# A fused attention and feed-forward layer: the five engines' instruction lists in a new order

## The reference

```python
x = x + xcond(layernorm(x), ctx, ctx, k_length)     # 8 heads, softmax over the 256 columns
x = x + ffn(layernorm(x), w_router, w_fc, w_proj)   # two experts, top one by a router

def xcond(q, k, v, k_length):
    s = SCALE * log(k_length)[:, None, None, None]
    attn = softmax(s * einsum('bhdq,bhdk->bhqk', qh, kh))
    return einsum('bhqk,bhdk->bhdq', attn, vh)

def ffn(x, w_router, w_fc, w_proj):
    logits = x @ w_router.T                           # 2 experts
    a = square(where(h >= 0, h, 0.5 * h))             # h = x @ w_fc[e].T, 1024 wide
    return a @ w_proj[e].T                            # of the chosen expert, times its probability
```

## Time and profile before

| | |
|---|---|
| median of 3 runs | 172.38 us (172.37 to 172.74) |
| profiled execution, span of its instructions | 170.4 us (its own time is not given apart from the three runs) |
| TensorE, busy | 161.4 us (95%) |
| VectorE, busy | 129.2 us (76%) |
| ScalarE, busy | 97.0 us (57%) |
| GpSimd, busy | 58.6 us (34%) |
| ACT_TABLE_LOAD | 1 of 1.28 us |

### The profile page before, as it was taken

How to read it: one execution, slowest core, us unless ns; L and a number is a source line. 1 busy time by engine, 2 the same in 40 slices (tenths; PEclk the granted TensorE clock), 3 DMA queues, 4 the chain that set the end, 5 groups by cost and what they waited for, 6 DMA issues and landing times.

```text
span 170.4 us, 4075 instructions
## 1 busy us (share of the span) xinstructions
PE 161.4 (95%) x1494; PEld 139.9 (82%) x1494; DVE 129.2 (76%) x301; ACT 97.0 (57%) x181; POOL 58.6 (34%) x68
## 2 busy tenths in 40 slices
PE   7998887899999989999989999999999999999992
PEld 7986745487698869896978798969879999999991
DVE  7799987999898999995999867953179875056442
ACT  4444979558659956957346526943794065335220
POOL 7331544630322420372521260405023253136330
PEclk9999999999999999999999999999999999999999
DMA  4577857794468054004501460002010000010001
GB/s 120 167 241 246 259 190 233 217 292 126 143 229 251 3 161 120 14 19 139 174 0 62 125 189 4 0 0 67 0 62 0 4 0 0 4 61 0 0 4 62
DMA packets 18883, 16.98 MB, mean 100 GB/s; under 512 B 1776, under 2 KB 18672, under 8 KB 18864
## 3 DMA queue, kind: packets, MB, share of 16 engines
q1 hardware_dynamic: 18144, 16.00, 30.3%
q10 hardware_dynamic: 720, 0.73, 1.5%
HBM read 8.72 MB, written 1.05 MB: 57 GB/s over the span
## 4 chain that ended last, share of the span: by engine, by line
PE 75%; DVE 11%; issue 4%; SPq 3%; ACT 3%; DMA 2%; DVEq 0%; ACTq 0%
PE hp L1358 25%; PE ops L1388 22%; PE pv L1342 6%; PE stp L1318 6%; PE ops L1273 5%; DVE negm L813 5%; PE snp L1265 3%; DMA x_raw<-x 2%; ACT probs L514 2%; DVE a_lo L921 2%; PE ops L1376 2%; PE pv L1376 1%; PE stp L1324 1%; PE pv L1398 1%; PE snp L1301 1%
## 5 line engine op out<-in xcount | busy, mean ns | idle before, releaser
L378 POOL TENSOR_TENSOR a_buf<-l_buf 128x512 f32<-128x512 f32 x32 | 35.7, 1119 | 77.8 <-DVE a_lo L921 44.6
L514 ACT ACTIVATE probs<-stp,scale_b 128x1024 f32<-128x1024 f32 x30 | 33.4, 1114 | 14.8 <-PE stp L1318 11.3
L1358 PE MATMUL hp<-xt_hi,wfc_hi 128*128 128x256 f32 x128 | 37.2, 291 | 0.0
L813 DVE TENSOR_REDUCE negm<-snp 128x4 f32<-128x1024 f32 x28 | 34.1, 1218 | 3.6 <-PE snp L1265 3.4
L1358 PE MATMUL hp<-xt_hi,wfc_lo 128*128 128x256 f32 x128 | 35.8, 279 | 0.0
L1358 PE MATMUL hp<-xt_lo,wfc_hi 128*128 128x256 f32 x128 | 35.7, 279 | 0.0
L522 ACT ACTIVATE l_buf<-hp 128x512 f32<-128x512 f32 x32 | 18.8, 594 | 23.7 <-PE hp L1358 17.0
L921 DVE TENSOR_TENSOR a_lo<-a_buf,a_hi 128x512 fp32r<-128x512 f32 x32 | 26.2, 831 | 7.6 <-ACT a_hi L529 6.2
L1358 PEld LDWEIGHTS hp<-xt_hi,wfc_hi 128*128 128x128 f32 x128 | 24.0, 188 | 2.1 <-issue 1.0
L1388 PE MATMUL ops<-wproj_hi,a_hi 128*128 128x256 f32 x112 | 23.6, 292 | 0.5 <-DVE wproj_lo L953 0.5
L1358 PEld LDWEIGHTS hp<-xt_hi,wfc_lo 128*128 128x128 f32 x128 | 24.1, 188 | 0.0
(11 more groups left out here) (112 smaller groups left out, 237.2 us busy)
## 6 DMA issues: line engine op xcount, KB each, us to landing
k_st<-k_hi SPq DMA_DIRECT2D x16, 128.0 KB, 2.1
wfc_raw<-w_fc_t SPq DMA_DIRECT2D x8, 256.0 KB, 4.4
wproj_raw<-w_proj_t SPq DMA_DIRECT2D x8, 256.0 KB, 3.5
q_st<-q_hi SPq DMA_DIRECT2D x14, 128.0 KB, 2.1
x_raw<-x SPq DMA_DIRECT2D x8, 128.0 KB, 3.0
k_st<-k_lo SPq DMA_DIRECT2D x8, 128.0 KB, 2.4
v_raw<-ctx_t SPq DMA_DIRECT2D x8, 128.0 KB, 2.6
x_keep<-x SPq DMA_DIRECT2D x8, 128.0 KB, 2.7
```

The lines of the kernel that those rows point to most:

```text
L378: pool.tensor_tensor(a_buf[d % 2][:, :, :], l_buf[d % 2][:, :, :], l_buf[d % 2][:, :, :], ALU.mult).then_inc(s_a, 1)
L514: act.activation(probs[g][:, :, :, :], pair[:, :, :].rearrange("p e (c n) -> p e c n", c=KC), ACT.Exp, scale=scale_b[:, b:b + 1]).then_inc ...
L813: dve.tensor_reduce(negm[b % 2][:, :, :, g].rearrange("p c e -> p e c"), pair[:, :, :].rearrange("p e (c n) -> p e c n", c=KC), AX.X, ALU. ...
L1358: last = pe.matmul(hp[:, d % 2, half], wfc[w][:, kc, c * P:(c + 1) * P], xt[:, kc, :], start=(c % 2 == 0 and kc == 0 and w == 0 and xt is ...
```

## The change

The entries of all five lists stand in another order; each entry stands in it once, as before. The core of the difference, by engine:

```diff
 # ACT
-            act.preload_act_table_set("natural_log_exp_and_others")
+            load_consts()
             load_kv(act, 0)
-            load_consts()
             load_kv(act, 1)
+            load_router()
             k_part_hi(0)
             x_ln(0)
             x_rstd(0)
             q_part_hi(0)
             x_ln(1)
+            len_log()
             x_rstd(1)
+            q_put()
             k_part_hi(1)
-            q_put()
+            k_part_hi(2)
             q_part_hi(1)
...
             max_rows(0)
             x_ln(2)
             x_rstd(2)
+            x_ln(3)
+            x_rstd(3)
             exp(0, 0)
-            x_ln(3)
-            split_w(0, 1)
-            x_rstd(3)
+            split_w(0, 2)
             exp(0, 1)
...
+            max_rows(1)
+            pick_keys()
+            k_part_hi(3)
             split_w(0, 3)
-            exp(0, 3)
+            x_ln(4)
+            x_rstd(4)
+            x_ln(5)
+            x_rstd(5)
+            exp(1, 0)
+            exp(1, 1)
+            exp(1, 2)
+            exp(1, 3)
+            y_ln(0)
+            y_rstd(0)
...
+            act.preload_act_table_set('natural_log_exp_and_others')
             leaky(3, 6)
+            square_hi(3, 6)
             leaky(3, 7)
-            square_hi(3, 6)
             square_hi(3, 7)
 # DVE
+            q_normalise(1)
             q_put()
-            q_normalise(1)
             row_max(0, 0)
 # PE
+            values(2, 0)
+            values(2, 1)
+            scores_qk(3, 3)
             ffn1(0, 0)
             ffn1(0, 1)
-            scores_kq(2, 3)
-            scores_qk(3, 3)
-            values(2, 0)
-            values(2, 1)
 # SP
             load_x(sp, 0)
             load_x(sp, 1)
+            load_weights(sp, 0, 0)
+            keep(0)
             stack_k(sp, 0, 0)
```

More of the change, by code:

```diff
@@ L572, in _ @@
             x_rstd(2)
+            x_ln(3)
+            x_rstd(3)
             exp(0, 0)
-            x_ln(3)
-            split_w(0, 1)
-            x_rstd(3)
+            split_w(0, 2)
             exp(0, 1)
+            exp(0, 2)
             q_part_hi(2)
-            split_w(0, 2)
-            exp(0, 2)
-            split_w(0, 3)
-            exp(0, 3)
+            q_part_hi(3)
+            exp(0, 3)
+            max_rows(1)
+            pick_keys()
+            k_part_hi(3)
+            split_w(0, 3)
+            x_ln(4)
[8 more added lines that the diff above has]
+            y_rstd(0)
             split_w(0, 4)
             split_w(0, 5)
[L585 to L591, removed]
             split_w(0, 6)
             q_part_hi(4)
[L594 to L600, removed]
             max_rows(2)
             split_w(0, 7)
-            x_rstd(5)
-            x_ln(6)
             exp(2, 0)
+            split_w(1, 0)
             y_ln(1)
@@ L608, in _ @@
             exp(2, 1)
+            k_part_hi(4)
+            k_part_hi(5)
+            exp(2, 2)
             xt_part_hi(0)
[L610 to L613, removed]
             exp(2, 3)
+            split_w(1, 1)
+            split_w(1, 2)
+            x_ln(6)
             leaky(0, 0)
             square_hi(0, 0)
-            q_part_hi(5)
[L618 to L622, removed]
+            max_rows(3)
+            leaky(0, 1)
+            square_hi(0, 1)
+            exp(3, 0)
+            split_w(1, 3)
+            q_part_hi(5)
             leaky(0, 2)
[L624 to L627, removed]
+            x_rstd(6)
             exp(3, 1)
             leaky(0, 3)
-            coef_exp(0)
-            split_w(1, 3)
-            square_hi(0, 3)
             exp(3, 2)
-            k_part_hi(5)
+            square_hi(0, 2)
             leaky(0, 4)
             exp(3, 3)
+            square_hi(0, 3)
+            y_ln(2)
+            y_rstd(2)
+            coef_exp(0)
+            k_part_hi(6)
             max_rows(4)
-            y_ln(2)
-            k_part_hi(6)
             split_w(1, 4)
+            split_w(1, 5)
             leaky(0, 5)
-            y_rstd(2)
             square_hi(0, 4)
-            split_w(1, 5)
+            exp(4, 0)
             y_ln(3)
-            square_hi(0, 5)
             y_rstd(3)
+            k_part_hi(7)
             leaky(0, 6)
-            exp(4, 0)
-            square_hi(0, 6)
             exp(4, 1)
@@ L653, in _ @@
             q_part_hi(6)
+            exp(4, 2)
+            square_hi(0, 5)
+            square_hi(0, 6)
+            leaky(0, 7)
             split_w(1, 6)
-            leaky(0, 7)
+            leaky(1, 0)
+            exp(4, 3)
+            max_rows(5)
+            split_w(1, 7)
+            x_ln(7)
+            x_rstd(7)
             square_hi(0, 7)
-            leaky(1, 0)
-            exp(4, 2)
+            square_hi(1, 0)
+            exp(5, 0)
             leaky(1, 1)
-            k_part_hi(7)
@@ L661, in _ @@
[L661 to L664, removed]
+            square_hi(1, 1)
             leaky(1, 2)
-            square_hi(1, 1)
-            q_part_hi(7)
-            exp(5, 0)
             square_hi(1, 2)
             exp(5, 1)
-            leaky(1, 3)
             exp(5, 2)
             exp(5, 3)
+            leaky(1, 3)
+            q_part_hi(7)
+            leaky(1, 4)
+            square_hi(1, 3)
+            y_ln(4)
+            y_rstd(4)
@@ L674, in _ @@
+            leaky(1, 5)
             coef_exp(1)
             max_rows(6)
[L676 to L681, removed]
+            y_ln(5)
             square_hi(1, 4)
-            y_ln(5)
-            y_rstd(5)
             square_hi(1, 5)
             leaky(1, 6)
+            y_rstd(5)
+            exp(6, 0)
+            xt_part_hi(2)
+            leaky(1, 7)
             exp(6, 1)
-            xt_part_hi(2)
@@ L689, in _ @@
             square_hi(1, 6)
-            leaky(1, 7)
+            square_hi(1, 7)
             exp(6, 2)
-            square_hi(1, 7)
             exp(6, 3)
-            coef_exp(2)
[L695 to L705, removed]
+            leaky(2, 0)
+            square_hi(2, 0)
@@ L706, in _ @@
+            max_rows(7)
+            exp(7, 0)
+            leaky(2, 1)
+            square_hi(2, 1)
+            leaky(2, 2)
+            exp(7, 1)
+            exp(7, 2)
+            exp(7, 3)
+            square_hi(2, 2)
+            y_ln(6)
+            coef_exp(2)
+            y_rstd(6)
             leaky(2, 3)
+            square_hi(2, 3)
             leaky(2, 4)
[L708 to L711, removed]
             square_hi(2, 4)
@@ L714, in _ @@
             y_rstd(7)
+            leaky(2, 5)
             xt_part_hi(3)
+            leaky(2, 6)
+            coef_exp(3)
             square_hi(2, 5)
-            leaky(2, 6)
+            square_hi(2, 6)
             leaky(2, 7)
-            square_hi(2, 6)
+            square_hi(2, 7)
             leaky(3, 0)
-            square_hi(2, 7)
-            coef_exp(3)
             square_hi(3, 0)
@@ L1576, in _ @@
             ffn2(1, 4)
-            ffn1(1, 11)
             ffn2(1, 5)
@@ L1626, in _ @@
             ffn2(2, 3)
+            ffn2(2, 4)
+            ffn1(2, 10)
+            ffn1(2, 11)
             ffn1(2, 12)
-            ffn2(2, 4)
             ffn1(2, 13)
+            x_transpose(3)
             ffn1(2, 14)
             ffn1(2, 15)
-            x_transpose(3)
             ffn2(2, 5)
@@ L1638, in _ @@
             ffn1(3, 2)
+            ffn1(3, 3)
             ffn2(2, 8)
```

574 lines of the change are left out of this document (285 added, 289 removed).

## The result

The changed kernel takes **207.32 us** (four runs, 206.40 to 208.09) against 172.52 us for the kernel before in the same comparison: **1.201 times** as long, interval 1.195 to 1.207, some 35 us. The forecast was 199 with a range of 187 to 231. The profiled execution of the changed kernel is the one of 208.09 us.

What follows compares the result with a forecast made beforehand. The prelude's chain through all engines, then PE's feed-forward matmuls, were taken to bound the kernel; 18.3 (prelude) + 5.2 (later waits) + 3 (PE's speed) = 26.5 on 172.4 gave 199 us, range 187 to 231, own bounds 192 to 207.

Steps and rivals of the forecast that it cites:

- The count and the price of the loads: On ACT: 34 table loads instead of one, 1.28 us each, 1.48 with its activation; busy time from 97.0 to about 139.
- The prelude, steps 1 to 5: Chain from layer norm to first `ffn1`, in five stretches: first `ffn1` at 63.2 against an equal point of 44.9, +18.3 us.
- some 15: Part of the prelude's 18.3 us put down to the table loads in it, in us.
- the rest: Part of the prelude's 18.3 us beyond the loads' share, put down to the new order itself.
- step 1: From the start to the first `row_max`: loads around the first `x_ln`, `x_rstd` pairs move it from 8.61 to 14.2, +5.6 us.
- PE's speed: PE's matmuls in the prelude may run slower after long waits: 3 us taken, at best 0, at most 6.8.
- I find two such places: Under feed-forward work, PE waits at `x_transpose(1)` (1.9 us) and `x_transpose(3)` (3.3): together +5.2, between 0 and 8.
- DVE may be the later one anyway: At the two late transposes, DVE rather than ACT might set the time, the reason for a lower bound of 0.
- Each load holds ACT longer: Rival: up to 1.52 us more behind each load on ACT, some 22 x 1.4 = 31 us more, 230 us; chance 0.18.
- Only the prelude pays: Rival: loads under feed-forward work hide, PE keeps its speed and regains 1.2 us of gaps, 189.5 us; chance 0.12.
- Not slower: Rival: every load runs in ACT's 73.4 us of idle time, or loads are not run, 172 us; chance 0.04.

Runs made afterwards that it cites:

- the late loads alone: New order with the right table preloaded at ACT's head and `exp_and_others` preloaded behind `exp(2,3)`, against the kernel before: 1.076 times, median 186.66 us.

## Why the prediction was right, and where it was off

Begin of the landmarks, us from the start of the span; the last line is the first `ffn1` or the equal point:

| | before | predicted | one load, new order | changed | changed, 53 more fillers |
|---|---|---|---|---|---|
| first `row_max` | 8.61 | 14.2 | 9.47 | 13.73 | 13.73 |
| `exp(0,0)` | 15.80 | 26.4 | 16.57 | 29.44 | 25.84 |
| `exp(1,0)` | 25.61 | 41.4 | 27.11 | 47.36 | 41.61 |
| `exp(2,0)` | 37.40 | 52.6 | 38.91 | 59.87 | 53.71 |
| first `ffn1` | 44.9 | 63.2 | 49.02 | 71.14 | 64.98 |

- **The count and the price of the loads** were right: 34 of 1.28 us, ACT busy 140.8 (forecast 139), and 1.51 us for a load with its activation (forecast 1.48).
- **The prelude, steps 1 to 5,** was right as a mechanism and, with the clock kept at 1.00, in size: the last column differs from the forecast by at most 1.8 us, 20.1 against 18.3 at the first `ffn1`. Of these, 18.0 are the loads ("some 15"), 2.1 the order ("the rest"). At the first pair (step 1) the order's share, by the kernel with one load, is 9.47 - 8.61 = 0.9 us, the loads' 13.73 - 9.47 = 4.3.
- **PE's speed** was the first term that was mis-sized: forecast 3, "at best 0", at most 6.8; 3.5 to 6.2 was measured. In the changed kernel PE waits 3.6 us for `q_hi`, then up to 5.0 us for `probs`, its granted clock goes to 0.50, and ten fillers take 4.22 us instead of 2.50. The first fillers of the earlier trace rows, from which the forecast had its ratio of 224 to 128, were slow at a clock that reads 1.00; why, no run shows. The choice of 3 rested on half of the pieces being slow; all of them from 10 to 20 us are, in the profiled execution.
- **"I find two such places"** is the step that failed, and the term that was mis-sized most: 5.2 us forecast, at most 8. The two were real and about right (1.66 us measured for 1.9, 2.54 for 3.3), but there are three more: `x_transpose(2)` 0.92, `ffn1` for `l_buf` 1.56, `ffn2` for `y` 0.75. The stretch lost 9.6 us, not 5.2, and the late loads 11.4 by the times. "DVE may be the later one anyway" did not hold. The list of ACT had been read for the transposes alone; the third kind of place is a `leaky` behind a pair of loads, with nothing on PE in between. Some 2 us of the 9.6, and 4 of the 11.4, are in no wait of PE over 0.7 us and stay open.
- **Sum:** 18.3 + 5.2 + 3 = 26.5 was forecast; by the profiles it is 20.1 + 6.2 + 9.6, rounded, of a span that grew by 35.8. All three terms were too small, and none made up for another. The median lies 0.3 us above the forecast's own bound of 207, inside its range. Those bounds are also added up wrongly: 0 to 8 and 0 to 6.8 on top of 172.4 + 18.3 give 190.7 to 205.5, not 192 to 207.
- **Each load holds ACT longer:** no. An activation begins 0.01 or 0.02 us behind the load (ACT's timeline above), and four loads taken out gave 5.4 us where they last 5.1. The Trainium skill, ScalarE: Activation LUTs, section What ACT_TABLE_LOAD costs, counts 1.38 us of drain behind each load, 2.66 us for a switch, by estimate 10.6 for four. The trace does not agree: here the next activation follows at once. The gap of 1.52 us in the earlier trace rows was the DMA's.
- **Only the prelude pays:** no, the late loads alone cost 11.4 us. **Not slower:** no, the 34 loads were run, and of ACT's 73.4 us of idle time 65.4 are still there: most of its waits did not lie where the loads stand. With only one load the same order takes 1.7 us more than before.

## What to carry to other kernels

A change that "only moves lines" is read from the built program: a line that sets a state for all that follows costs nothing to move in the list and here 33 instructions in the build. An added piece on an engine with room is priced by stage: in a chain through all engines it counts about in full (5.4 us for four loads of 1.28), under a saturated engine in part (11.4 us for 17 of them, 21.8 us of ACT's time), and there each entry of the waiting engine must be gone through, not only the conspicuous ones. When a chain grows by waits of TensorE, look at the granted clock of the longer version, since work that fitted before may now also run slower: 4.22 us instead of 2.50 for ten fillers here.

## What was not expected

More work made the kernel faster: 53 products that nobody reads, 4.1 us less, with the granted clock at 1.00 instead of 0.50 from 10 to 20 us. Nearly the same number of loads cost 32.9 us in the new order (33) and 38.1 in the old one (31), so the order that loses 1.7 us with one load is the better one with many. And moving one activation out of PE's way made the kernel 2.9 us slower: it moved the wait, and in the profiled execution the clock fell behind it.
